# A decoder of two layers: three slots of stacks, eight buffers of weights, maxima one period ahead, a unit's products with the values in one block

## What is computed

```python
x = x + _L0_attn_ref(_layernorm(x))        # softmax attention, 16 heads of 16
x = x + _L0_xattn_ref(_layernorm(x), ctx)  # softmax attention to the 120 rows of context
x = x + _L0_ffn_ref(_layernorm(x))         # linear layer, weights quantised to 4 bits, plus LoRA
x = x + _L1_attn_ref(_layernorm(x))        # RMS norm, rotary embedding, sigmoid weights divided by their sum
x = x + _L1_xattn_ref(_layernorm(x), ctx)  # one head of 256
x = x + _L1_ffn_ref(_layernorm(x))         # two experts for each 128 rows, chosen by a hash of their mean
```

## Time and profile before

| | |
|---|---|
| median of three runs | 1116.27 us (1112.7 to 1116.56) |
| the profiled execution | 1116.71 us |
| its span | 1114.8 us |
| TensorE busy | 1038.1 us, 93% |
| TensorE weight loads (beside it) | 800.2 us, 72% |
| VectorE busy | 780.9 us, 70% |
| ScalarE busy | 636.5 us, 57% |
| GpSimd busy | 590.0 us, 53% |

### The profile page before, as it was taken

The page is one execution under the profiler, slowest core; times in us unless marked ns, Lnnn a source line. Parts: engine busy times, 40 slices in busy tenths (PEclk is TensorE's granted clock), DMA queues, the critical chain, the costliest instruction groups (busy, mean ns, idle before and its releaser), DMA issues.

```text
span 1114.8 us, 24383 instructions
## 1 busy us (share of the span) xinstructions
PE 1038.1 (93%) x8490; PEld 800.2 (72%) x8490; DVE 780.9 (70%) x1748; ACT 636.5 (57%) x1160; POOL 590.0 (53%) x924
## 2 busy tenths in 40 slices
PE   5689999999989999999999999999999999988976
PEld 4456777777767777777777777777777767877864
DVE  4577788788777556666677878878788744568772
ACT  2335666666656666666664556666666676654430
POOL 3343444555545545555666988778787711134340
PEclk9889999999999999999999999999999999999989
DMA  6986676565656346754451756556566680045446
GB/s 194 120 100 95 99 104 92 95 88 73 93 75 81 61 79 93 121 93 93 93 69 21 101 71 86 86 70 85 77 83 88 85 94 8 15 126 159 140 151 207
DMA packets 123626, 104.94 MB, mean 94 GB/s; under 512 B 26841, under 2 KB 123241, under 8 KB 123497
## 3 DMA queue, kind: packets, MB, share of 16 engines
q1 hardware_dynamic: 117794, 99.71, 55.3%
q10 hardware_dynamic: 5712, 3.68, 1.5%
HBM read 29.47 MB, written 4.19 MB: 30 GB/s over the span
## 4 chain that ended last, share of the span: by engine, by line
PE 80%; DVE 9%; DMA 4%; issue 3%; SPq 2%; ACT 2%; POOL 1%; ACTq 0%; DVEq 0%; POOLq 0%
PE l_o L1077 13%; PE l_ring L1142 11%; PE l_sT L1061 11%; PE l_copy L1123 8%; PE l_ring L1092 7%; PE l_ring L1179 7%; PE l_copy L1100 4%; PE l_ring L1162 3%; DVE l_nmax L915 3%; PE l_ring L1190 2%; PE l_sT L1720 2%; DMA qstack<-l_qpart 2%; PE l_copy L1170 1%; PE l_sT L1744 1%; DVE l_tokk L936 1%
## 5 line engine op out<-in xcount | busy, mean ns | idle before, releaser
L714 ACT ACTIVATE l_probs<-l_sT 128x1024 f32<-128x1024 f32 (+1 forms) x320 | 322.7, 1024 | 119.4 <-PE l_sT L1061 74.0
L915 DVE TENSOR_REDUCE l_nmax<-l_ring 128x2 f32<-128x512 f32 (+1 forms) x384 | 249.9, 675 | 106.6 <-PE l_ring L1092 101.2
L1061 PE MATMUL l_sT<-qstack,kstack 99*128 99x256 bf16 (+2 forms) x1280 | 184.4, 272 | 1.1 <-ACT l_probs L714 1.1
L1077 PE MATMUL l_o<-l_probs,v_heads 128*32 128x256 f32 (+1 forms) x2560 | 158.5, 383 | 0.0
L1092 PE MATMUL l_ring<-kstack,qstack 96*128 96x256 bf16 (+1 forms) x1024 | 140.0, 249 | 19.8 <-DMA qstack<-l_qpart 6.3
L1061 PEld LDWEIGHTS l_sT<-qstack,kstack 99*128 99x128 bf16 (+2 forms) x1280 | 126.6, 104 | 24.7 <-ACT l_probs L714 2.0
L1092 PEld LDWEIGHTS l_ring<-kstack,qstack 96*128 96x128 bf16 x1024 | 75.5, 98 | 76.4 <-DVE l_nmax L915 23.2
L1142 PE MATMUL l_ring<-wT,l_zT 128*128 128x256 f32 x512 | 126.4, 385 | 3.5 <-DVE l_tokk L936 2.6
L1077 PEld LDWEIGHTS l_o<-l_probs,v_heads 128*32 128x32 f32 (+1 forms) x2560 | 72.8, 109 | 57.2 <-issue 17.0
L573 POOL TENSOR_SCALAR factors<-mv 128x2 f32<-128x2 f32 (+1 forms) x77 | 17.5, 227 | 177.5 <-DVE mv L972 151.4
L1142 PEld LDWEIGHTS l_ring<-wT,l_zT 128*128 128x128 f32 x512 | 90.9, 190 | 23.4 <-issue 13.6
(11 more groups left out here) (200 smaller groups left out, 1875.2 us busy)
## 6 DMA issues: line engine op xcount, KB each, us to landing
qstack<-l_qpart SPq DMA_DIRECT2D x288, 128.0 KB, 4.2
kstack<-l_kpart SPq DMA_DIRECT2D x192, 128.0 KB, 5.1
kstack<-in_experts SPq DMA_DIRECT2D x36, 256.0 KB, 3.1
kstack<-l_kpart SPq DMA_DIRECT2D x96, 60.0 KB, 3.3
qstack<-in_experts SPq DMA_DIRECT2D x20, 256.0 KB, 3.1
out_y<-x_res SPq DMA_DIRECT2D x16, 256.0 KB, 3.8
l_cx<-in_ctx SPq DMA_DIRECT2D x32, 90.0 KB, 3.1
x_res<-in_x SPq DMA_DIRECT2D x1, 2048.0 KB, 15.7
```

The source lines that it names most:

```text
L714: act.activation(probs[g % 4][0:kp, :], sT[g % 2][0:kp, :], ACT.Sigmoid if sig(u) else ACT.Exp, scale=HD ** -0.5).then_inc(p_ok, 1)
L915: dve.tensor_reduce(nmax[u % 2][:, tt, h0:h0 + hb], bank("s", u, i)[:, 0:hb * sk].rearrange("p (h k) -> p h k", h=hb), AX_X, ALU.max, nega ...
L1061: i = pe.matmul(sT[g % 2][0:kp, j * S:(j + 1) * S], kstack[u % SLOTS][0:rows_used, col * width(u) + kt * kp:col * width(u) + (kt + 1) * kp ...
L1077: i = pe.matmul(o_bank[32 * j:32 * (j + 1), group % 2, :], v[u % 2][0:kp, kt, 4 * group + j, :], probs[g % 4][0:kp, j * S:(j + 1) * S], st ...
```

## The change

The stacks have three slots instead of four, and there are eight buffers of exponentials instead of four (`PROBS`). In the two softmax layers the maxima are made one period ahead instead of two, projections and splits two ahead, rows three; the sigmoid layer keeps its leads. All four groups `pv0` to `pv3` of a unit are done in the next period, in one block, and the second half of them goes into the copy bank (`outputs_bank`), so that `pv2` waits for an empty copy bank and the next job of the copy bank for the copy of the outputs. The transposed maxima of unit p are made in period p itself. The lists of jobs are new. In the tail the bank of the hash is free as soon as VectorE has copied the projection (`hash_out`); the buffers of the experts take other halves. The diff, cut:

```diff
...
 CHUNKS = B * TT
-SLOTS = 4
+SLOTS = 3
+PROBS = 8
 W_NAMES = ["in_q", "in_k", "in_v", "in_o", "x_q", "x_k", "x_v", "x_o", "l_q", "l_k", "l_v", "l_o"]
...
     "self": """
-        sT0 p0q qa dq0 s sT1 s qb np s s pv2 e0 pv3 o1 e1 s s ka s kb p0k dk0 p1q oT1 sT2 e2 dq1 p2q dq2 sT3 e3 nT p1k
-        dk1 s p2k dk2 lo l1 l2 va q0 rows vb s pv0 pv1 o0 s aT s s sT4 e4 s z cl e5 oT0 ws qm q1 sT5 s qA sT6 e6 fac xs
-        xb s w pa cx e7 st xf pb s lw lf sT7 qB""",
+        qa qb pv0 pv1 pv2 l1 pv3 o0 oT0 o1 oT1 nT s s s aT p0q np dq0 p0k s s s e0 e1 sT0 s lo p1q sT1 dq1 s ka kb sT2
+        q0 rows e2 p1k e3 p2q s pa dk0 pb s sT3 qA sT4 va st vb dk1 e4 z dk2 dq2 s lw cl sT5 fac lf s e5 w qB s cx xb s
+        xs sT6 s p2k e6 e7 sT7 s q1 ws xf l2 qm""",
     "cross": """
-        p0q np t.w sT0 qa qb s sT1 pv2 p0k e0 pv3 o1 s e1 s ka kb dq0 s oT1 dq1 dk1 sT2 p1q nT va fr dk0 vb p1k p2q
-        rope_q s rope_k aT e2 sT3 dq2 s rows s p2k fxb fz dk2 pv0 pv1 cx o0 e3 xb cl pa fac pb ffac qT st fa fb oT0 z
-        fst s kT""",
+        qa fr qb o0 o1 np pv0 rope_q pv1 pv2 pv3 p0q t.w dk0 oT0 nT oT1 ka s kb p1q p0k s s aT s s p1k sT0 cx s sT1 va
+        rope_k p2q e0 rows vb dq2 st dq1 cl e1 fz fxb dq0 pa pb sT2 z fac fst xb s sT3 p2k e2 qT fa dk2 fb ffac kT dk1
+        s e3""",
     "sigmoid": """
-        qa sT0 qb rope_q sT1 p0q dq0 pv2 e0 pv3 ka kb rope_k o1 e1 sT2 p1q oT1 e2 dq1 p0k dk0 va fr dq2 e3 vb rows dk1
-        p2q sT3 pv0 pv1 o0 aT p2k dk2 sT4 fxb sT5 st p1k fz e4 pa z pb e5 xb fac ffac fst sT6 qT e6 fa fb oT0 sT7 e7 kT""",
+        rope_q p0q qa dk1 dq2 qb pv0 pv1 fr o0 p1q o1 pv2 e0 pv3 oT0 e1 sT0 oT1 dq0 e2 sT1 p0k ka p1k kb sT2 aT va dk0
+        sT3 rows st e3 vb fz rope_k sT4 p2q pa fxb e4 z e5 fst sT5 pb qT sT6 dk2 fa e6 xb sT7 dq1 fb fac p2k ffac kT e7""",
 }
...
     "dq1:0 p1k:0 dk2:0 qa:1 qb:1 p2q:0 dq2:0 p2k:0 dq0:1 p0q:1 ka:1 kb:1 p0k:1 dk0:1 rows:2 z:2 xs:2 p1q:1 dq1:1 "
-    "p1k:1 dk1:1 dk2:1 l0 va:0 vb:0 s:0 p2q:1 dq2:1 p2k:1 s:0 qa:2 qb:2 s:0 p0q:2 dq0:2 ka:2 s:0 kb:2 p0k:2 dk0:2 "
-    "s:0 rows:3 s:0 p1q:2 s:0 dq2:2 dq1:2 p1k:2 s:0 dk1:2 z:3 s:0 s:0 s:0 s:0 s:0 s:0 s:0 s:0 np:0 s:1 p2q:2 s:1 "
-    "dk2:2 p2k:2 xf:2 nT:0")
+    "p1k:1 dk1:1 dk2:1 l0 va:0 vb:0 s:0 p2q:1 dq2:1 p2k:1 s:0 s:0 s:0 s:0 s:0 s:0 s:0 s:0 s:0 s:0 s:0 s:0 s:0 s:0 "
+    "s:0 np:0 xf:2 nT:0")
 FIRST_PERIOD = (
...
+    "s:1 s:1 dq0:2 qa:2 s:1 qb:2 e:0:0 s:1 sT:0:0 s:1 ka:2 s:1 rows:3 s:1 dk0:2 kb:2 p1q:2 e:0:1 sT:0:1 s:1 p1k:2 "
+    "sT:0:2 e:0:2 dk2:2 s:1 sT:0:3 p0q:2 p0k:2 p2k:2 s:1 va:1 dq2:2 e:0:3 vb:1 e:0:4 sT:0:4 s:1 z:3 s:1 e:0:5 "
+    "sT:0:5 e:0:6 p2q:2 dq1:2 s:1 s:1 sT:0:6 s:1 e:0:7 dk1:2 sT:0:7 s:1")
 
...
 LATE = 10
-LEAD = {"sT": 0, "e": 0, "pv": 0, "va": 1, "vb": 1, "nT": 1, "np": 1, "s": 2, "qa": 3, "qb": 3, "ka": 3, "kb": 3, "rope_q": 3,
-        "rope_k": 3, "z": 4, "rows": 4, "xb": 4, "cx": 4, "cl": 5, "qT": 3, "kT": 3, "o1": -1, "oT1": -1, "aT": -1,
-        "pa": -1, "pb": -1, "st": -2, "fac": -2, "o0": 0, "oT0": 0}
+
+LEAD = {"sT": 0, "e": 0, "pv": -1, "o": -1, "oT": -1, "aT": -1, "pa": -1, "pb": -1, "st": -2, "fac": -2, "va": 1, "vb": 1,
+        "np": 0, "nT": 0, "s": 1, "qa": 2, "qb": 2, "ka": 2, "kb": 2, "z": 3, "rows": 3, "xb": 3, "cx": 3, "cl": 4,
+        "p0": 2, "p1": 2, "p2": 2, "dq": 2, "dk": 2}
+LEAD_SIGMOID = {"qa": 3, "qb": 3, "ka": 3, "kb": 3, "rope_q": 3, "rope_k": 3, "qT": 3, "kT": 3, "z": 4, "rows": 4, "xb": 4}
 FFN = {"fr": 0, "fxb": 0, "fz": 0, "fa": 0, "fb": 0, "fst": -1, "ffac": -1}
...
 
-def split_unit(p):
-
-    if p + 3 < 2 * B:
-        return p + 3
-    return p + 2 if p + 2 >= 2 * B else None
+def units_of(word, job, p):
+
+    soft = LEAD.get(word, LEAD.get(job, LEAD.get(job[0:2])))
+    sigmoid = LEAD_SIGMOID.get(word, soft)
+    out = []
+    if soft is not None and 0 <= p + soft < 2 * B:
+        out.append(p + soft)
+    if 2 * B <= p + sigmoid < UNITS:
+        out.append(p + sigmoid)
+    return out
 
...
             continue
...
+        units = units_of(word, job, p)
+
+        if job in ("qa", "ka") and len(units) == 2:
+            units = units[0:1]
+        for u in units:
+            its = kind_of(u)
+            if job == "s":
+                i = seen["s"]
+                seen["s"] += 1
+                if i < maxima_of(u):
+                    out.append((job, u, i))
+                continue
...
+            if job in ("qb", "kb") and len(units) == 2 and its == "sigmoid":
+                out.append((job[0] + "a", u, 0))
+            out.append((job, u, i))
     return out
...
                 ring[job, u, i] = len(ring)
-    copied = {}
+
+    copied, copies_before, outputs_before, last_outputs = {}, {}, {}, None
     for p in PERIODS:
         for job, u, i in ORDER[p]:
-            if job in ("z", "fz", "cx", "nT", "aT", "qT", "kT", "w", "qA") or job in ("qb", "kb") and kind_of(u) != "sigmoid":
+            if (job, i) == ("pv", 2):
+                copies_before[u], last_outputs = len(copied), u
+            opens = job in ("z", "fz", "cx", "nT", "aT", "qT", "kT", "w", "qA") or job in ("qa", "ka") and kind_of(u) != "sigmoid"
+            if opens:
+                outputs_before[job[0] + "b" if job in ("qa", "ka") else job, u] = last_outputs
+            if opens and job not in ("qa", "ka") or job in ("qb", "kb") and kind_of(u) != "sigmoid":
                 copied[job, u, i] = len(copied)
...
-        probs = [sb(f"probs{i}", [P, 4 * S], F32) for i in range(4)]
+        probs = [sb(f"probs{i}", [P, 4 * S], F32) for i in range(PROBS)]
         o_sb = [sb(f"o{i}", [P, 2, S], F32) for i in range(2)]
...
             return chunk["sT", u, chunks_of(u) - 1]
+
+        def outputs_bank(half):
+            return copy_bank[:, :].rearrange("p (g s) -> p g s", g=2) if half else o_bank[:, :, :]
 
...
                 act.wait_ge(sT_ps, g + 1)
-                if g >= 4:
-                    act.wait_ge(pv_ps, pv[pv_of(g - 4)] + 1)
+                if g >= PROBS:
+                    act.wait_ge(pv_ps, pv[pv_of(g - PROBS)] + 1)
                 kp = SC if kind_of(u) == "cross" else P
-                act.activation(probs[g % 4][0:kp, :], sT[g % 2][0:kp, :], ACT.Sigmoid if sig(u) else ACT.Exp,
+                act.activation(probs[g % PROBS][0:kp, :], sT[g % 2][0:kp, :], ACT.Sigmoid if sig(u) else ACT.Exp,
                                scale=HD ** -0.5).then_inc(p_ok, 1)
...
                     act.wait_ge(ring_full, ring["oT", u - 1, half] + 1)
-                act.activation(o_sb[half][:, :, :], o_bank[:, :, :], ACT.Identity).then_inc(o_ok, 1)
+                act.activation(o_sb[half][:, :, :], outputs_bank(half), ACT.Identity).then_inc(o_ok, 1)
 
...
             def copy_slot(job, u):
-                n = copied[job, u, 0]
+                n, outputs = copied[job, u, 0], outputs_before[job, u]
                 if n >= 1:
                     pe.wait_ge(copy_empty, n)
+                if outputs is not None:
+                    pe.wait_ge(o_ok, 2 * outputs + 2)
                 return copy_bank
...
                     pe.wait_ge(ring_empty, ring["vb", u, 0] + 1)
-                if group % 2 == 0 and (u, group) != (0, 0):
-                    pe.wait_ge(o_ok, 2 * u + group // 2)
+                if group == 0 and u > 0:
+                    pe.wait_ge(o_ok, 2 * u - 1)
+                if group == 2:
+                    if u > 0:
+                        pe.wait_ge(o_ok, 2 * u)
+                    pe.wait_ge(copy_empty, copies_before[u])
                 per = chunks_of(u) // 4
...
                     for j in range(4):
-                        i = pe.matmul(o_bank[32 * j:32 * (j + 1), group % 2, :], v[u % 2][0:kp, kt, 4 * group + j, :],
-                                      probs[g % 4][0:kp, j * S:(j + 1) * S], start=(group % 2 == 0 and kt == 0),
+                        i = pe.matmul(outputs_bank(group // 2)[32 * j:32 * (j + 1), group % 2, :], v[u % 2][0:kp, kt, 4 * group + j, :],
+                                      probs[g % PROBS][0:kp, j * S:(j + 1) * S], start=(group % 2 == 0 and kt == 0),
                                       stop=(kt == per - 1), skip_group_check=True)
...
             dve.wait_ge(v_ps, v_no("hash", g) + 1)
-            link(dve.tensor_copy(proj, v_bank[0:PER, 0:NB]))
+            dve.tensor_copy(proj, v_bank[0:PER, 0:NB]).then_inc(hash_out, 1)
+            dve.wait_ge(hash_out, g + 1)
             dve.scalar_tensor_tensor(weights, proj, 0.0, powers, ALU.is_gt, ALU.mult)
...
             if last[0] == "hash":
-                pe.wait_ge(picked_ok, last[1] + 1)
+                pe.wait_ge(hash_out, last[1] + 1)
             for k in range(KT):
...
             if before[-1][0] == "hash":
-                pe.wait_ge(picked_ok, g)
+                pe.wait_ge(hash_out, g)
             for k in range(KT):
...
```

45 lines of the change are left out of this document (14 added, 31 removed), and 18 rows, old and new, of tables (DRAIN, FIRST_PERIOD).

## The result

The changed kernel takes 1150.72 us (1147.6 to 1154.41, four runs) against 1115.89 for the kernel before on the same chip: 1.031 times as long, 95% interval 1.028 to 1.034. The profiled execution took 1154.41 us with a span of 1152.5. Forecast was 1127 with a range up to 1146: the sign was right, the size was not, 35 us instead of 11.

What follows compares the result with a forecast made beforehand. TensorE was taken as the bound in the layers, the opening excepted. From 1116.7 us: +9.8 (opening and self attention), +5 cross, -4 sigmoid, -2.4 tail, +2 seams gave 1127, range 1101 to 1146.

Steps and rivals of the forecast that it cites:

- Part 1: Opening: maxima steps follow each other, period 1 begins at 71 instead of 87.66, -16.7 us; 7.5 of work owed later.
- Part 2: Self attention: TensorE waits for VectorE's reductions with two ring banks; period 22.4 us against 20.90; standing +9.8 with the opening.
- nearly hidden: Self attention: the maxima row's DMA starts at 8.2, lands in 2.5 us, is wanted at 10.2; at 5.5 it costs 3.
- upper bound of 23.6: Self attention: the period in us if the DMA of the maxima is late.
- the walk: Job-by-job count of a self-attention period from its start: 22.1 us, with 0.3 added for scatter 22.4.
- VectorE's idle stretch: Self attention: VectorE stands five us during the block of products, from about 1 to 6.1, before reductions resume.
- Rival (a): Self attention: TensorE stays the bound, periods remain 20.9 us; 1106, or 1099 with the whole tail gain; chance 0.25.
- +1.5 for each of 14 periods: Self attention: the loss in us for every period with sixteen maxima steps, periods 1 to 14.
- Part 3: Cross attention: first `s` waits 0.6 to 1 us for late k stacks; 14.5 against 14.07, 12 periods, +5.
- Part 4: Sigmoid layer: new order and one switch less; walk gives 19.4 against 19.97; -0.4 for 10 periods, -4 us.
- Part 5: Last layer: values' product starts 1.71 us earlier, but the next waits for VectorE's bias; 0.4 left, six times, -2.4.
- Rival (c): DMAs miss the one-period lead: maxima rows +1.0 us each, stacks in cross attention +0.7; 1149; chance 0.18.

Runs made afterwards that it cites:

- np_first_nt_early: Changed kernel with the maxima's split moved up on GpSimd and their transposition ahead of the second half of the values' products: 1144.98 us, 1.026 of before.
- np_first_dq_late: np_first with SyncE issuing the next unit's first three stack DMAs only once the period's first scores are done: 1136.05 us, 1.018 of before.
- hybrid: Kernel before up to unit 32, changed kernel's order, slots, buffers and tail from the first sigmoid unit on: 1093.68 us, 0.980 of before.
- hash_before: Kernel before with only the tail's edit: the bank of the hash is free once its projection is copied: 1106.58 us, 0.992 of before.
- after_dq_late: Changed kernel with SyncE issuing the next unit's first three stack DMAs only once the period's first scores are done, in self attention: 1140.05 us, 1.022 of before.
- np_first: Changed kernel with GpSimd's split of the maxima moved up right behind the last reduction it needs, in self attention: 1184.74 us, 1.063 of before.
- qm_moved: Changed kernel with GpSimd's maximum over partitions (`qm`) moved from the end of period 11 to behind the maxima's split: 1148.63 us, 1.028 of before.
- half_max_after: Changed kernel with VectorE reducing only the first half of the keys in self attention's maxima steps: 1144.42 us, 1.025 of before.

## Why the prediction was wrong, step by step

**Part 1, the opening.** Right as far as it went. `nT` is copied at 55.24, forecast 54.7, and period 1 begins at 72.06, forecast 71. Of the 5.6 us that the table misses, 2.7 are only a matter of the mark: with the forecast's own 71 and 10.2 the first scores of unit 1 come at 81.2, while -9.2, with the whole 7.5 owed in it, stands for 78.5. The other 2.8 are real: the period begins 1.1 later, and its first scores come at 84.03, 12.0 us into it and not 10.2. They wait 1.48 us there.

**Part 2, self attention.** The failed step is one sentence: "I take 2.5, since it is a small transfer: nearly hidden." The 2.5, counted from the end of the issue, was nearly right, 2.6 in the period shown. What failed is "nearly hidden". By the prediction's own numbers the row lands at 10.7 and is wanted at 10.2; this half microsecond was put at nothing in the 22.4, and the landing was taken as the row's own affair and the clock as full throughout. From the start of the issue the scores follow after 3.2 to 3.3 us with the stack DMAs on the way, 3.6 to 3.8 in some periods, 3.0 without them and 4.9 to 5.1 when they leave together. Quiet periods were 23.0 against the forecast's 22.4, and those with a fallen clock 24.4 to 26. Taking the meeting away returns 11.8 of the 14.0 us by which the ten periods had been underrated, 3.4 of idle time and 8.4 of longer busy time, mostly from the clock. The upper bound of 23.6 has no working behind it: with the 3 us that the prediction itself gives for a landing of 5.5, it would be 25.4.

Without the meeting the period is 22.6, near the walk's 22.4, and what is left above 20.9 is waits of `s` and of the transposes for VectorE, as the walk has them. But VectorE's idle stretch is less of a price than the walk made it. Filling it took the period from 23.4 to 22.5 in np_first_nt_early's order, of which 0.5 was `pv2` waiting for the copy of `nT`; np_first_dq_late has 22.5 with the stretch unfilled. Halving the reductions brought 0.4 more. Rival (a) fell with this too: TensorE did not stay the bound, for reasons beside the one it named.

**Periods 11 and 12**, 13 us: missing altogether. The step that failed is "+1.5 for each of 14 periods": all were taken to be like the quiet period 6, whose rows the walk used. The two pauses of 6 and 7 us around `qm` could be seen in the trace of before, at 312 to 326, and a one-period lead puts `np` behind them. The 40 slices of before show them too: TensorE is at eight tenths in the twelfth (307 to 334 us), where "Time and profile before" has nine or more from the fourth slice on.

**Part 3, cross attention.** The wait named is there: the first `s` of a unit after its stacks, 0.3 to 1.1 us, in some periods. The profile names no releaser for this one, but the last of the stack DMAs ahead of it landed at 561.91.

```profile
562.00 0.37 PE L1111 MATMUL l_ring<-kstack,qstack 96*128 96x120 bf16 x4 [0.99 <-issue]
```

The sum was +5 and the stretch is +15.7. Over the ten periods from unit 16, the stretches are 140.68 us (busy 137.89) before and 151.16 (busy 142.77) after: 5.6 more idle, 4.9 more busy, with the clock at 0.99 and low in one period. Another 5.7 us come in periods 28 to 31 (72.61 to 78.32), where a period projects two units. No run took this apart.

**Part 4, sigmoid layer.** Right sign, size off by a factor of nearly four: -1.0 per period (19.98 to 18.99), not -0.4, and -15.1 with the last four periods. TensorE idled 3.4 us of 266.0 and now 1.0 of 250.9; the other 12.6 are busy time (some of it moved across the marks: 2214 products lie between them before, 2195 after). A part of it is again pauses that the length of a product covers: nine periods with the same 1476 products take 179.8 us before and 170.9 after, and in them steps of over 0.28 us from start to next start occur 54 times before and 18 times after. What the products wait for there was not measured. hybrid shows that the gain is this layer's own. A walk by start-to-start times of single steps misses what steps cost in another order.

**Part 5, the tail.** The edit is worth 8.9 us alone, against 2.4. The step that failed: "the product with them (1033.53) waits for that". In hash_before this product starts 0.6 us ahead of the addition; that the row at 1033.53 stood behind 1032.63 was the order in time and no wait. With that corrected the term is the whole 1.71 six times, 10.3, the bound of -10 that the prediction wrote down.

**Rival (c)** gave 1149, with 0.18: nearest to the measured time. Its mechanism, a row of maxima late in a pipeline shorter by one period, is the one that after_dq_late took out, but with the clock that falls behind it it is 11 of the 35 us; the rest of (c)'s sum is matched by causes it did not name.

## What to carry to other kernels

A small DMA on the path is priced by what else is in flight when it is issued, so before shortening a lead, list every transfer that leaves within its landing time; holding bulk transfers back until the small one's reader has started can be worth more than issuing them early. A lead shortened by one stage also removes the cover of every rare pause in the queues it passes, so look for the longest gap of each queue, and not only at a quiet period. And the profile's busy time hides waits: a product ahead of one counts in full, so compare orders from start to next start. And when a change has gains and losses in separate stretches, run the stretches apart: here the losing 3% held a winning 2%.

## What the runs showed of the hardware

- A 24 KB DMA of 51 packets from ScalarE's queue: its reader starts 3.0 us behind its issue alone (after_dq_late), 4.9 to 5.1 with three stack DMAs of 128 KB issued from SyncE within the same microsecond (np_first). Its packets take 1.4 us of engine time alone and 4.3 then, and 4.2 in the kernel before, where nobody waits for them.
- GpSimd's maximum over partitions is shown with 0.38 to 0.41 us, and with pauses of 5.46 to 5.91 before and 6.98 to 7.15 behind it in three kernels (before, after, qm_moved): some 13 us in which its queue does little else.
- The granted clock fell from 2.4 to 1.2 GHz (0.5 in the records) behind waits of the first scores of 0.5 to 2 us in several periods, and did not in the same periods once the wait was gone (np_first 0.953, np_first_dq_late 0.983 over the run). Not every such wait brings it: in half_max_after two such waits of 1.0 to 1.1 us, in periods that follow each other (from 246.86 and 269.90), have the clock at 1.00 behind them.
- A product of `s` is 0.27 us long in the profile, and the next one starts 0.12 us after it when nothing holds it. A wait for it therefore costs some 0.15 us more than the idle time shown, and one shorter than that shows no idle time at all.
